# First attention pass from four partial products, two heads at a time on row groups of TensorE

## The reference, cut to what matters

```
x_h = x.reshape(b, t, h, d).transpose(0, 2, 1, 3)              # h = 16, d = 8
xw  = einsum('bhtd,hde->bhte', x_h, w_att_val)
att = softmax(einsum('bhte,bhse->bhts', xw, x_h) / sqrt(d))
o   = einsum('bhts,bhsd->bhtd', att, vx);  return o @ out_w.T + out_b
```

## Time and profile before

| | us |
|---|---|
| median of 3 runs (3308.93 to 3323.37) | 3321.49 |
| the profiled execution | 3324.53 |
| its span in the trace | 3322.7 |

### The profile page before, as it was taken

The page is one execution under the profiler, slowest core; times in us unless marked ns, Lnnn a source line. Parts: engine busy times, 40 slices in busy tenths (PEclk is TensorE's granted clock), DMA queues, the critical chain, the costliest instruction groups (busy, mean ns, idle before and its releaser), DMA issues.

```text
span 3322.7 us, 84797 instructions
## 1 busy us (share of the span) xinstructions
PE 3023.1 (91%) x34588; PEld 1880.2 (57%) x34588; DVE 2424.8 (73%) x4986; ACT 2329.6 (70%) x4768; POOL 1226.8 (37%) x778
## 2 busy tenths in 40 slices
PE   5899698989999999999999999999999999999876
PEld 5279446555565656565555656565655556565644
DVE  6722577868787878778687878787787878787743
ACT  4453387877777777878777776778787777777744
POOL 1133043443333333444433332434444333333433
PEclk9699699999999999999999999999999999999988
DMA  5446101101010111110010101111100101011000
GB/s 141 116 139 184 39 28 35 26 27 27 24 43 24 36 29 35 32 35 26 19 36 23 43 24 36 29 35 32 35 26 22 32 24 43 24 36 28 9 10 4
DMA packets 128575, 134.10 MB, mean 40 GB/s; under 512 B 18100, under 2 KB 111070, under 8 KB 128190
## 3 DMA queue, kind: packets, MB, share of 16 engines
q1 hardware_dynamic: 123648, 119.37, 12.9%
q0 software_dynamic: 4544, 9.32, 1.3%
HBM read 81.06 MB, written 30.28 MB: 34 GB/s over the span
## 4 chain that ended last, share of the span: by engine, by line
PE 54%; DVE 19%; ACT 9%; issue 4%; POOL 2%; DMA 1%; SPq 1%; POOLq 0%; ACTq 0%; DVEq 0%
PE bank L1482 6%; PE bank L2066 6%; PE bank L1496 4%; PE bank L724 4%; PE bank L1466 4%; PE bank L2110 3%; PE bank L2052 3%; DVE turn_f L2239 3%; PE bank L2042 3%; PE bank L2033 2%; PE bank L1768 2%; PE bank L2005 2%; ACT area L2128 2%; DVE nmax_a L1612 2%; DVE ss L2232 2%
## 5 line engine op out<-in xcount | busy, mean ns | idle before, releaser
L1553 ACT ACTIVATE prob_a<-bank 128x512 f32<-128x512 f32 x1024 | 560.7, 603 | 127.4 <-PE bank L1496 122.1
L1612 DVE TENSOR_REDUCE nmax_a<-bank 128x1 f32<-128x512 f32 x768 | 497.1, 683 | 71.0 <-PE bank L1466 68.7
L1972 POOL TENSOR_TENSOR rn<-ss,minus_half 128x16 f32<-128x16 f32 x128 | 396.3, 3096 | 278.6 <-DVE ss L2234 275.4
L1995 POOL TENSOR_TENSOR rs_f<-rs_f,minus_half 128x4 f32<-128x4 f32 x32 | 33.0, 1032 | 1041.7 <-DVE rs_f L1347 1041.7
L1978 POOL TENSOR_TENSOR turn_f<-turn_f 128x512 f32<-128x512 f32 x256 | 325.2, 1291 | 196.4 <-DVE turn_f L2239 196.3
L2128 ACT ACTIVATE area<-bank 128x512 f32<-128x512 f32 x640 | 353.1, 605 | 58.7 <-PE bank L2066 48.5
L1496 PE MATMUL bank<-Qst_a,Kst_a 74*128 74x512 bf16 x1024 | 375.2, 389 | 13.8 <-DVE nmax_a L1612 6.5
L1466 PE MATMUL bank<-Kst_a,Qst_a 72*128 72x512 bf16 x768 | 301.7, 393 | 15.5 <-ACT prob_a L1553 6.4
L2239 DVE TENSOR_TENSOR turn_f<-area,rotf 128x1024 f32<-128x1024 f32 x256 | 303.4, 1216 | 7.8 <-POOL area L1982 6.8
L1482 PE MATMUL bank<-prob_a,V_a 128*18 128x512 f32 x2048 | 275.7, 611 | 19.1 <-ACT prob_a L1553 17.8
L1982 POOL TENSOR_TENSOR area<-turn_f,rn 128x1024 f32<-128x1024 f32 x128 | 243.9, 1905 | 18.4
(11 more groups left out here) (304 smaller groups left out, 6819.6 us busy)
## 6 DMA issues: line engine op xcount, KB each, us to landing
Qst_a<-dq_a SPq DMA_DIRECT2D x192, 96.0 KB
Kst_a<-dk_a SPq DMA_DIRECT2D x192, 96.0 KB
area<-in_W SPq DMA_DIRECT2D x25, 512.0 KB, 4.6
dq_a<-prob_a SPq DMA_DIRECT2D x80, 128.0 KB
V_f<-in_W SPq DMA_DIRECT2D x14, 512.0 KB, 4.5
dk_a<-prob_a SPq DMA_DIRECT2D x48, 128.0 KB
ys_d<-otok_f SPq DMA_DIRECT2D x39, 128.0 KB, 3.6
x_a<-in_x_in SPq DMA_DIRECT2D x16, 256.0 KB, 2.8
```

Source lines behind the costliest of these rows:

```text
L1553: nc.scalar.activation(dst, bk.full(act, product)[rows, :], func, **kw).then_inc(a_emptied["act"], 1)
L1612: nc.vector.tensor_reduce(out=nmax_a[:, g, t, j:j + 1], in_=bk.full(dve, f)[:], op=ALU.max, axis=AX.X, negate=True).then_inc(emptied, 1)
L1972: nc.gpsimd.tensor_tensor(rn[:, t % 2], ss[:, t % 2], minus_half[:], ALU.pow).then_inc(f_root, 1)
```

## The change

**First pass.** Two further tiles, `Q4_a` and `K4_a` (128 partitions, a ring of two), hold for each of the four heads of a group 32 partitions: four products of parts (Q parts 1, 0, 0, 1 against K parts 0, 1, 0, 1) with 8 features each. The first pass multiplies 32 x 128 by 32 x 512 from there. Matmuls come in pairs: heads 0 and 1 of one query tile, then heads 2 and 3, on neighbouring row groups of 32; PE takes both banks before it issues the first of the two. The order of the first pass is now query tile outside, head inside. The second pass keeps its 74 rows of nine products.

**DMAs.** The spill writes 12 parts of 128 KB (7 for Q, 5 for K) where it wrote 8, since the two layouts need different orders of parts. `load_fours` adds two DMAs a group, issued before the stack loads, as soon as the last first pass of the group two before is done. PE waits for them (`a_four`) before the first pass of a group, and for the stack (`a_stack`) only before the second.

**Order.** All of `TIMES` and `SEATS` are drawn anew; `OPEN` and `STEP` stay. In PE's streams and in the plan of the banks an odd-numbered first pass takes the slot of the even one before it.

**Scratch.** The program is built with `dynamic_dma_scratch_size=8192`.

```diff
-        dq_a, dk_a = scratch("dq_a", [H0, 2 * SPLIT - 1, D0, T]), scratch("dk_a", [H0, SPLIT, D0, T])
+        Q_PARTS, K_PARTS, STACK_AT = (1, 0, 0, 1, 2, 0, 1), (0, 1, 0, 1, 2), 2
+        dq_a, dk_a = scratch("dq_a", [H0, len(Q_PARTS), D0, T]), scratch("dk_a", [H0, len(K_PARTS), D0, T])
+        Q4_a, K4_a = sb("Q4_a", [P, RING, T], BF16), sb("K4_a", [P, RING, T], BF16)
...
-        first = [[("first", g, j, t) for j in range(4) for t in range(NT)] for g in range(G)]
+        first = [[("first", g, j, t) for t in range(NT) for j in range(4)] for g in range(G)]
...
-            for c in range(2 * SPLIT - 1):
-                sp.dma_start(dq[:, c], parts_q[:, c % SPLIT, :]).then_inc(s, 16)
-                if c < SPLIT:
-                    sp.dma_start(dk[:, c], parts_k[:, c, :]).then_inc(s, 16)
+            for d, parts, picked in ((dq, parts_q, Q_PARTS), (dk, parts_k, K_PARTS)):
+                for c, part in enumerate(picked):
+                    sp.dma_start(d[:, c], parts[:, part, :]).then_inc(s, 16)
...
+        def load_fours(sp, g):
+            for tile, d in ((Q4_a, dq_a), (K4_a, dk_a)):
+                sp.dma_start(tile[:, g % RING, :], d[4 * g:4 * g + 4, 0:4].rearrange("h c d t -> h (c d) t")).then_inc(a_four[g], 16)
...
+        def first_pair(r, pe, bk, g, n):
+
+            if n == 0:
+                pe.wait_ge(*nth(r, a_four[g], FOURS))
+            pair = [(bk.take(pe, f), f) for f in first[g][n:n + 2]]
+            for ps, (_, _, j, t) in pair:
+                rows = slice(32 * j, 32 * j + 32)
+                nc.tensor.matmul(ps[:], Q4_a[rows, g % RING, t * P:(t + 1) * P], K4_a[rows, g % RING, :], start=True, stop=True)\
+                    .then_inc(a_filled, 1)
...
-                    yield A_GROUP[g] + 1.2 * n
-                    if g + 1 < G:
-                        first_pass(g + 1, n)
+                    if g + 1 < G and n % 2 == 0:
+                        yield A_GROUP[g] + 1.2 * n
+                        first_pair(r, pe, bk, g + 1, n)
                     yield A_GROUP[g] + 1.2 * n + 0.4
                     if n == 0:
+                        pe.wait_ge(*nth(r, a_stack[g], STACKED))
                         pe.wait_ge(*nth(r, a_mrow[g], 16))
...
-    nc = bacc.Bacc("TRN2", target_bir_lowering=False, num_devices=1)
+    nc = bacc.Bacc("TRN2", target_bir_lowering=False, num_devices=1, dynamic_dma_scratch_size=8192)
```

More of the change, by code:

```diff
@@ L259 @@
+            "a": ((14, 33.4, 34, 36, 56, 59, 83),
+                  (-216.2864, -216.28639, -214.38803, -199.25144, -194.05611, -173.52494, -165.61867)),
             "finish": ((14.7, 15.7),
-                       (-67.57821, -66.57821))},
+                  (-127.69294, -126.69294))},
         "gpsimd": {
             "gate": ((0, 1),
-                     (-53.54468, -52.54468)),
+                  (-72.86371, -71.86371)),
             "b": ((0.5, 1.5),
-                  (-44.93433, -43.93433)),
+                  (-60.10126, -59.10126)),
@@ L388 @@
+            "head": ((4.6, 6.1, 29.05),
[24 rows of a table added]
             "feed": ((6.175, 8.3, 8.55, 9.05, 9.55),
-                     (-116.73057, -106.30141, -103.55657, -103.17137, -100.22011)),
+                  (-119.00943, -106.2755, -102.64431, -101.83139, -101.82653)),
             "finish": ((11.2, 12.2),
-                       (-63.94697, -62.94697))},
+                  (-56.65509, -55.65509))},
         "vector": {
             "gate": ((113, 113.2, 113.4),
[9 rows of a table removed]
-            "head": ((1, 1.2, 1.5, 6.2, 6.5, 6.6, 6.7, 6.8, 16, 16.7, 17.4, 18.1, 18.8, 19.5, 20.2, 20.9, 21.6,
[31 rows of a table removed]
[6 rows of a table added]
@@ L435 @@
+            "head": ((1, 1.2, 1.5, 6.2, 6.5, 6.6, 6.7, 6.8, 16, 16.7, 17.4, 18.1, 18.8, 19.5, 20.2, 20.9, 21.6, 22.3, 23, 23.7, 24.4, 25.1, 25.8, 26.5, 28),
[17 rows of a table added]
             "feed": ((6.55, 6.8, 7.1, 8.8, 9.3, 9.8, 10.725),
-                     (-112.76509, -111.65438, -110.77237, -103.08967, -101.79345, -99.4833, -77.78949)),
+                  (-112.44282, -111.94019, -111.06759, -105.42364, -103.16781, -97.63035, -65.58373)),
             "finish": ((13.2, 13.4, 13.6),
-                       (-58.22573, -55.4072, -53.6288))}}
+                  (-44.95523, -35.74576, -32.46602))}}
@@ L439 @@
 SEATS = {
-    "a": ("154203542054415324103240512302323131245140035540350301020350225305431052431501305310130014"
-          "53201152051051023103150350342"),
-    "b": "550243503111500034533453305032530452",
-    "head": "32010321541515105430",
-    "f": ("321401341540154325031214124541423451224254512415544510520151430123510545402503420312434212"
-          "4312012042141403"),
-    "feed": "433230540"}
+    "a": ("322531453051021052310415320140512143014251053314203145021302123012523540125340310343143042"
+          "35102023545234353512132115153"),
@@ L447 @@
+    "b": "334532453410543020114515002343554031",
+    "head": "23231152051425201435",
+    "f": ("524142312540341502534205014345401304125205123151200503420441405130130542503243024140243532"
+          "5140325341231244"),
+    "feed": "004354024"}
 B_AT = 5
@@ L1273, in mixer_kernel @@
         a_x_in, a_xn, a_split, a_spill = (sem(n) for n in ("a_x_in", "a_xn", "a_split", "a_spill"))
-        a_stack = [sem(f"a_stack{g}") for g in range(G)]
+        a_stack, a_four = ([sem(f"{n}{g}") for g in range(G)] for n in ("a_stack", "a_four"))
         a_mparts, a_mrow = sem("a_mparts"), [sem(f"a_mrow{g}") for g in range(G)]
@@ L1293, in mixer_kernel @@
         f_tanh, f_out, f_stored = sem("f_tanh"), sem("f_out"), sem("f_stored")
-        first = [[("first", g, j, t) for j in range(4) for t in range(NT)] for g in range(G)]
+        first = [[("first", g, j, t) for t in range(NT) for j in range(4)] for g in range(G)]
         second = [[("second", g, k, j) for k in range(NT) for j in range(4)] for g in range(G)]
         plan_head = [(4.5, "xnT", ["act"]), (6, "xw", ["act"]), (6, "v", ["dve"])]
-        plan_head += [(16 + 0.7 * n, f, ["dve"]) for n, f in enumerate(first[0])] + [(29, ("mT", 0), ["act"])]
+        plan_head += [(16 + 0.7 * (n - n % 2), f, ["dve"]) for n, f in enumerate(first[0])] + [(29, ("mT", 0), ["act"])]
         plan_a = []
@@ L1304, in mixer_kernel @@
             for n in range(16):
-                if g + 1 < G:
-                    plan_a.append((A_GROUP[g] + 1.2 * n, first[g + 1][n], ["dve"]))
+                if g + 1 < G and n % 2 == 0:
+                    plan_a += [(A_GROUP[g] + 1.2 * n, f, ["dve"]) for f in first[g + 1][n:n + 2]]
                 plan_a.append((A_GROUP[g] + 1.2 * n + 0.4, second[g][n], ["act"]))
@@ L1383, in load_stack @@
             for i in range(SPLIT):
-                sp.dma_start(Qst[rows * i:rows * i + rows], q_rows[D0 * i:D0 * i + rows]).then_inc(s, 16)
-                sp.dma_start(Kst[rows * i:rows * i + rows], k_rows).then_inc(s, 16)
+                at = D0 * (STACK_AT + i)
+                sp.dma_start(Qst[rows * i:rows * i + rows], q_rows[at:at + rows]).then_inc(s, 16)
+                sp.dma_start(Kst[rows * i:rows * i + rows], k_rows[D0 * STACK_AT:D0 * STACK_AT + rows]).then_inc(s, 16)
         def max_to_stack(sp, mT, Qst, landed):
@@ L1420, in head_sync @@
                 if attended:
+                    sp.wait_ge(*bk.made(first[G - RING + g][-1]))
+                load_fours(sp, g)
+                if attended:
                     sp.wait_ge(*bk.made(second[G - RING + g][-1]))
@@ L1425, in head_sync, with a_sync @@
             max_to_stack(sp, mT_a[:, 0, :], Qst_a[:, 0], a_mrow[0])
-        def a_sync(r, sp, bk):
+        def a_sync(r, sp, bk, hk):
             for g in range(G):
@@ L1432, in a_sync @@
                     max_to_stack(sp, mT_a[:, g % 2, :], Qst_a[:, g % RING], a_mrow[g])
+                else:
+                    sp.wait_ge(*hk.made(first[0][-1]))
+                    load_fours(sp, RING)
+                if g + 1 + RING < G:
+                    yield A_GROUP[g] + 18.4
+                    sp.wait_ge(*bk.made(first[g + 1][-1]))
+                    load_fours(sp, g + 1 + RING)
                 if g + RING < G:
@@ L1448, in head_tensor @@
             last.then_inc(a_filled, 1)
-            for n, f in enumerate(first[0]):
-                _, _, j, t = f
+            for n in range(0, 16, 2):
                 yield 16 + 0.7 * n
-                if n == 0:
-                    pe.wait_ge(*nth(r, a_stack[0], STACKED))
-                nc.tensor.matmul(bk.take(pe, f)[:], Qst_a[0:STACK, 0, j, t * P:(t + 1) * P],
-                                 Kst_a[0:STACK, 0, j, :], start=True, stop=True).then_inc(a_filled, 1)
+                first_pair(r, pe, bk, 0, n)
             yield 29
@@ L1460, in a_tensor @@
         def a_tensor(r, pe, bk, hk):
-            def first_pass(g, n):
-                _, _, j, t = f = first[g][n]
-                if n == 0:
-                    pe.wait_ge(*nth(r, a_stack[g], STACKED))
```

(4 more changed lines are left out.)

30 lines of the change are left out of this document (18 added, 12 removed), and 229 rows, old and new, of the table TIMES.

## The result

The changed kernel takes 3454.25 us (median of 4 runs, 3440.26 to 3461.64) against 3322.43 (3308.93 to 3328.09): ratio 1.0397, 95% interval 1.0371 to 1.0422. It is slower by 4%, outside the predicted range and with the other sign.

What follows compares the result with a forecast made beforehand. PE was taken as the bound, busy 171.0 of 181 us a stage. 15 rows x -2.9 = -43.5 and opening +0.8 gave -43, so 3280 us; the range leaving out 2 in 10 was 3215 to 3345.

Steps and rivals of the forecast that it cites:

- Pairs and changes of shape: First pass on PE: 32 pairs save 6.9 us a row; 44 more changes of shape at 0.09 cost 4.0 us.
- The net of 2.9 us: PE's work in each row: 6.9 us saved by pairing less 4.0 us for changes of shape, times 15 rows.
- pairs that don't run side by side: Rival for first-pass pairs: no streaming saved, 44 changes of shape paid, +60 us, 3385; chance 0.04.
- a free change of shape: Rival for PE's matmuls: changing shape costs nothing, so the full 104 us is gained, about 3220; chance 0.05.
- PE is the bound: Steady stages: PE busy 171.0 of 181 us with 10 us idle, so the gain is PE time per stage.
- idle time moves by less than 3 us: Sign to check in a stage: the prediction is wrong if PE's idle time moves over 3 us either way.
- In the stages the head's 16 first passes are spread through the body, so nothing: Row heads: group 0 starts 0.8 us later after the split, costed at nothing in stages, +0.8 in the opening.
- costing the transfers at nothing: Eight further loads and four spills, 1.5 MB a row, meet DMA engines only 12% busy.
- The opening: Row 0 on three banks: pairs wait for reduction and exponential, 0 to +5 us, taken 0; load +0.8.
- Bank waits: Two banks per pair: close re-takings rise from 11 to 16 of 290; costed at nothing, bounds -3 to +7 us a row.
- The rival of the pair's second bank: First pass: PE waits 0.68 us for a second bank under reduction; ten such pairs a row give 3380; chance 0.19.
- Clock: Rival for the stages: more run at clock 0.96, taking 188 us for 181; ten more give 3350, five 3315; chance 0.08.

Runs made afterwards that it cites:

- e15: e14 with first passes contracting 32 stack rows on alternating row groups, which leaves part of the products out of the maxima: 3363.1 us, ratio 1.0103.
- e14: e3 again: the changed kernel's order, seats and pairs, with 72-row first passes from the stack, 8 spills, no partial products: 3363.1 us, ratio 1.0116.
- e18: e12 again, run beside e17, with 32-row pairs, eight loads a group and four more spills: 3342.7 us, ratio 1.0005.
- e17: e6 with e12's opening, leaving only the new order and seats of the stages against the kernel before: 3348.3 us, ratio 1.0017.
- e10: e2 again on another chip: the changed kernel with load_fours as eight DMAs of 32 rows: 3416.6 us, ratio 1.025.
- e11: e8 again: e10 with the first pass's eight parts spilled first, group 0's loads next, and banks taken singly: 3373.8 us.
- e3: The changed kernel with 72-row first passes from the stack, 8 spills and no partial products; order, seats and pairs kept: 3365.4 us, ratio 1.0116.
- e6: e3 with each first pass taking its bank by itself: 3357.1 us, ratio 1.0001.
- e7: e2 with the first pass's eight parts spilled first, group 0's loads next, other spills and stacks last: 3362.5 us, ratio 1.0024.
- e8: e7 with each first pass of a pair taking its bank by itself: 3364.1 us, ratio 1.0025.
- e12: e11 with row 0 as in the kernel before: single 72-row first passes, 8 spills, no loads of partial products: 3352.0 us, ratio 1.0067.
- e4: The kernel before with dynamic_dma_scratch_size=8192 alone: 3329.8 us, ratio 1.001.
- e16: The kernel before with each product's bank chosen again from its own trace, order kept (231 seats differ): 3412.2 us, ratio 1.024.
- e2: The changed kernel with load_fours as eight DMAs of 32 rows instead of two of 128: 3416.1 us, ratio 1.028.
- e5: e3 with first passes contracting 32 stack rows on alternating row groups, leaving part of the products out of the maxima: 3363.8 us, ratio 1.0021.

## Why the prediction was wrong

**Pairs and changes of shape: right.** A pair starts together and has the length of one; what follows starts 0.31 to 0.32 after it, and a pair starts 0.31 after a second pass (changed kernel):

```profile
1598.11 0.38 PE L1449 MATMUL bank<-Qst_a,Kst_a 74*128 74x512 bf16 x1
1598.42 0.39 PE L1398 MATMUL bank<-K_a,Q_a 32*128 32x512 bf16 x2
1598.74 0.60 PE L1449 MATMUL bank<-Qst_a,Kst_a 74*128 74x512 bf16 x2
```

That is 0.22 and 0.09 as taken. The count of changes was right: the traces have 138 in a stage of the changed kernel and 94 before, 44 more. The net of 2.9 us of PE's work a row measured 1.9 (e15 against e14) and 2.6 (e18 against e17), with more time at 1.2 GHz in e15 and e18. The rivals of pairs that don't run side by side and of a free change of shape are out.

**"PE is the bound": the first step that failed.** From 10 us of idle time in a stage I made PE's work the price of the stage. e15, which differs from e14 in the operands alone, shows PE's idle time rising by as much as its busy time falls, 1.9 us a stage. In e18 against e17, where loads and spills differ too, idle time took 1.6 of 2.6. DVE (146 of 185 us) and ACT (139) empty the banks, and PE, in order, meets them earlier if it works less. The change's 2.9 us x 15 = 43.5 were worth 0 us (e14 and e15, five runs each) and 6 us (e17 and e18, twelve each). Of the 2.9 in e15 the clock took about 1.0, by the estimate above, and the waits 1.9. The prediction was that idle time moves by less than 3 us; in the changed kernel it moved by 9.

**"In the stages the head's 16 first passes are spread through the body, so nothing": the dear one.** I had the 0.8 us of later start right in kind and let it be hidden. It was sized wrong as well: in the rows shown 12 spills took 9.0 us of SP in place of 5.1, not 2.5 more, and the loads landed 6.8 us after their issue. The group came 19.7 us after the first spill in place of 15.9. PE stood there in 11 of the 13 stages with everything behind it, 4.0 of the 8.9 us by which its idle time in a stage grew. e10 (30.6 us) and e11 (42.7) took 73 us back, more than half of the loss. My reason for costing the transfers at nothing, engines at 12%, was a mean over all engines; it says nothing of one transfer's time to land.

**The opening: mechanism right, size off.** Taken 0 to +5 and 0.8 for the load; measured 21. The missing term is SP's queue, where stores of 1 MB and the loads for groups 1 and 2 stand ahead of the maxima's transfer (11 us). The other half is first passes in twos on three banks: e3 and e14, without partial products, still start row 1 at 371.7 and 374.5, and e6, which takes its banks singly, at 371.2.

**Bank waits.** The rival of the pair's second bank had the right sign and a time of 3345 to 3380, but e7 against e8 shows nothing in taking both banks at once. What the new order costs by itself is e17 against before: 0.17%, with an interval across zero, in a group where before stood at 3340; against 3325 it would be 23 us. e12's remaining 24 us are of that size. The traces speak for a cost of the order: every kernel with the new timetables whose group 0 comes as early as before has a stage of 184.4 to 186.5 us, paired or not, where the kernel before has 183.1 and e4 183.9. Between these the share of the timetables stays open. Pairs in the old order weren't run.

**Clock.** In the stages the granted clock went from 0.99 to 0.97, which is 11.3 us a stage at 1.2 GHz in place of 5.3, worth some 3 us of PE's work. It came back to 0.98 with the waits (e11, 6.3 us), so most of the 3 us goes with the waits. A smaller part goes with the pairs themselves, as e14 and e15 show. I had it as a rival with 0.08; it added to the loss.

**Sum.** Of 3447 - 3328 = 119 us, 30.6 are the loads' few queues, 42.7 the spill ahead of group 0, 21.8 the opening, and 24 remain, in which pairing has a gain of 0 to 6 us. No kernel here beats the one before: of those with the change's pairs e18 is the nearest, at 1.0005 (0.998 to 1.003), and e6, without them, is at 1.0001 (0.998 to 1.002).

## What to carry to other kernels

Before costing a saving on the busiest engine, ask what that engine would meet next; here 10 us of scattered stalls in 181 were a loop of three engines and no slack. A transfer that the first product of a group needs has a latency of spill, landing, issue and landing; count it link by link against the old one, and issue what is needed first, first. Put many rows outermost on both sides of a DMA.

## What was not expected of the hardware

An issue on SP's queue took 0.38 us in quiet parts, 0.75 each in a burst of 12 spills, and 3.6 to 9.3 (for two) behind stores of 1 MB. Other bank seats alone lost 2.4% (e16, 1.9 to 3.0) without one operation added. Kernels with 32-row pairs were granted a lower clock than their 72-row partners (e15 0.953 to 0.956, e14 0.957 to 0.965), while PE was busy less. The kernel before had medians from 3325 to 3355 over the five groups, on one and the same chip 3355 and 3326, while the repeated kernels e2 and e10, e3 and e14, e5 and e15 agreed within 2.3 us, and e8 and e11, e12 and e18 within 10; what makes it wander is open.
